# Two attentions with keys on partitions: the second shift products follow the scores at once, and keys are spread one batch ahead

## What is computed

```python
# first: 32 batches, 128 queries, 120 keys, 16 heads of 8 channels
attn = jnp.einsum('bhqd,bhkd->bhqk', q, k) * scale
attn = jnp.clip(attn, -CLAMP, CLAMP)
attn = jax.nn.softmax(attn, axis=-1)
...
x = jnp.einsum('bhqk,bhkd->bqhd', attn, v).reshape(B, Nq, Cq)
return x @ Wo + bo

# second: 128 queries, 128 keys, 16 heads of 4 channels, causal
scores = jnp.einsum('bhqd,bhkd->bhqk', q, k) / jnp.sqrt(jnp.float32(HD))
scores = jnp.where(causal, scores, -jnp.inf)
attn = jax.nn.softmax(scores, axis=-1)
o = jnp.einsum('bhqk,bhkd->bhqd', attn, v).transpose(0, 2, 1, 3).reshape(b, s, L)
x = x + o @ w_up
```

## Time and profile before

| | |
|---|---|
| median of 3 runs | 2061.7 us (2058.45 to 2063.37) |
| the profiled execution, its time | 2061.81 us |
| its span in the profile | 2060.0 us, granted TensorE clock 0.928 |
| TensorE busy (weight loads) | 1802.4 us, 87% (1398.8, 68%) |
| VectorE busy | 1510.3 us, 73% |
| GpSimd busy | 1177.6 us, 57% |
| ScalarE busy | 1112.8 us, 54% |

### The profile page before, as it was taken

How to read it: one execution, slowest core, us unless ns; L and a number is a source line. 1 busy time by engine, 2 the same in 40 slices (tenths; PEclk the granted TensorE clock), 3 DMA queues, 4 the chain that set the end, 5 groups by cost and what they waited for, 6 DMA issues and landing times. The chain is left out here.

```text
span 2060.0 us, 40382 instructions
## 1 busy us (share of the span) xinstructions
PE 1802.4 (87%) x12276; PEld 1398.8 (68%) x12306; DVE 1510.3 (73%) x3109; ACT 1112.8 (54%) x2864; POOL 1177.6 (57%) x1241
## 2 busy tenths in 40 slices
PE   3678767799999999986999999997778887799998
PEld 2355546588888888864888888885444444588886
DVE  5698868677787787777666666666668886677876
ACT  1366645555555555543666666664346565555554
POOL 3666637467776777654333333334767773677764
PEclk9799976799999999985999999998879997699999
DMA  5111100455565555410000000000000000212222
GB/s 122 46 44 40 42 25 11 113 137 138 144 144 145 125 148 145 128 60 3 5 4 3 4 4 3 4 3 1 0 1 1 0 0 16 60 61 83 81 63 71
DMA packets 99991, 114.77 MB, mean 56 GB/s; under 512 B 18448, under 2 KB 55504, under 8 KB 99888
## 3 DMA queue, kind: packets, MB, share of 16 engines
q1 hardware_dynamic: 96960, 112.14, 20.6%
q10 hardware_dynamic: 2928, 1.39, 0.3%
HBM read 101.82 MB, written 3.28 MB: 51 GB/s over the span
## 5 line engine op out<-in xcount | busy, mean ns | idle before, releaser
L76 POOL TENSOR_TENSOR b_moe_hid_low<-b_moe_hid,b_moe_hid_high 128x512 fp32r<-128x512 f32 x256 | 331.9, 1296 | 172.0 <-ACT b_moe_hid_high L1027 168.4
L1033 ACT ACTIVATE bank<-bank 128x512 f32<-128x512 f32 x384 | 223.5, 582 | 341.3 <-PE bank L83 341.3
L1729 POOL TENSOR_TENSOR c_prob<-c_prob,c_recip 128x480 f32<-128x480 f32 x128 | 126.3, 987 | 294.0 <-DVE c_recip L1877 294.0
L1835 ACT ACTIVATE c_prob<-bank,c_shift 128x120 f32<-128x120 f32 x512 | 177.9, 360 | 169.7 <-DVE c_shift L1869 169.7
L1058 DVE TENSOR_TENSOR b_moe_gu<-bank,XC 128x512 f32<-128x512 f32 x256 | 176.7, 690 | 114.8 <-PE bank L83 99.0
L76 POOL TENSOR_TENSOR e_moe_hid_low<-e_moe_hid,e_moe_hid_high 128x512 fp32r<-128x512 f32 x128 | 165.9, 1296 | 83.5 <-ACT e_moe_hid_high L1027 82.8
L71 DVE CAST c_ts_high<-bank 128x480 fp32r<-128x480 f32 x128 | 84.2, 658 | 153.2 <-PE bank L1760 153.2
L1063 DVE TENSOR_TENSOR b_moe_hid<-bank,b_moe_gu 128x512 f32<-128x512 f32 x256 | 177.0, 691 | 8.9 <-POOL b_moe_hid_low L76 0.3
L1027 ACT ACTIVATE b_moe_hid_high<-b_moe_hid 128x512 fp32r<-128x512 f32 x256 | 159.7, 624 | 9.8 <-DVE b_moe_hid L1063 9.0
L1760 PE MATMUL bank<-c_cs,mT 96*128 96x120 f32 x1024 | 142.2, 283 | 6.2 <-POOL c_wvp_low L76 4.8
L1760 PEld LDWEIGHTS bank<-c_cs,mT 96*128 96x128 f32 x1024 | 132.8, 196 | 20.8 <-DVE c_ts_low L76 9.7
(11 more groups left out here) (372 smaller groups left out, 5490.4 us busy)
## 6 DMA issues: line engine op xcount, KB each, us to landing
XC<-b_comb SPq DMA_DIRECT2D x256, 256.0 KB, 4.3
XC<-e_comb SPq DMA_DIRECT2D x64, 256.0 KB, 3.1
X<-in_x SPq DMA_DIRECT2D x4, 512.0 KB, 9.1
a_att_qs_high<-XC SPq DMA_DIRECT2D x32, 64.0 KB, 1.8
a_att_qs_low<-a_Q_low SPq DMA_DIRECT2D x32, 64.0 KB, 1.9
a_att_ks_high<-a_K_high SPq DMA_DIRECT2D x32, 64.0 KB, 1.9
a_att_ks_low<-a_K_low SPq DMA_DIRECT2D x32, 64.0 KB, 1.9
b_moe_w_gate<-in_b_wgT SPq DMA_DIRECT2D x8, 256.0 KB, 2.8
```

What stands on the lines that cost most here:

```text
L76: return eng.tensor_tensor(low.bitcast(F32R), x, high, ALU.subtract)
L1033: act.activation(gate_b[j % 4][:], gate_b[j % 4][:], ACT.Silu).then_inc(s_silu, 1)
L1729: pool.tensor_tensor(prob[k][:], prob[k][:], recip[:, k, :].unsqueeze(2).broadcast_to([P, HG, NKV]), ALU.mult).then_inc(s_norm, 1)
L1835: i = act.activation(prob[k][:, h, :], score_b[g % 2][:, h * NKV:(h + 1) * NKV], ACT.Exp, bias=shift[:, k, h:h + 1], accum_out=sums[:, k, ...
```

## The change

On TensorE shift B moves up to stand directly behind the second phase, the projection comes next and the turn of the heads last before the values products. The turned heads now go to `side_b`, columns 256 to 383, instead of `out_b`. So the values products wait for the heads to have been read (`s_heads`) and no longer for the copy of the turned ones; the turn of the row maxima, which writes the same bank as the turned heads, waits for last round's copy; and VectorE's addition, which reads that bank, waits for this round's copy. The projection now comes behind a wait for the spread row maxima of its own round, which it had before as well.

On ScalarE exponential B and the copy of turned heads change places. On GpSimd the low parts and `kd` are taken out of batch b's part and put in front of it for batch b+1; those of batch 0 come ahead of the loop.

```diff
+                    def spread_keys(b, v):
+                        if clamp:
+                            pool.wait_ge(s_place[v], (b - v) * 16 + 64)
+                        else:
+                            low_parts(b, v)
+                            pool.wait_ge(s_low, b + 1)
+                        wait(pool, s_second, b - 1)
+                        for part in range(2):
+                            i = pool.tensor_tensor(kd[v % 2][part][:].bitcast(F32R),
...
+                        i.then_inc(s_kd, 1)
+                    spread_keys(0, 0)
                     def body(b, v):
                         u = v % 2
+                        if has(b + 1):
+                            spread_keys(b + 1, (v + 1) % 4)
                         if has(b):
-                            if clamp:
-                                pool.wait_ge(s_place[v], (b - v) * 16 + 64)
...
                             wait(pool, s_first, b + 1)
...
                         if has(t - 1):
                             pe.wait_ge(s_mz, mz_steps * t)
                             wait(pe, s_out, t - 5)
+                            wait(pe, s_headT, t - 4)
                             pe.transpose(side_b[:, 0:P], mz[1 - u][:], ident[:]).then_inc(s_mt, 1)
...
-                        if has(t - 4):
-                            pe.wait_ge(s_heads, t - 3)
-                            pe.transpose(out_b[:, 0:P], heads[u][:], ident[:]).then_inc(s_ht, 1)
+                        if has(t - 2):
+                            pe.wait_ge(s_inB, t - 1)
+                            shift(u, (2, 3)).then_inc(s_shB, 1)
+                        if has(t - 1):
+                            pe.wait_ge(s_mrow, t)
                         if has(t - 5):
                             pe.wait_ge(s_headT, t - 4)
                             wait(pe, s_out, t - 5)
-                            if has(t - 1):
-                                pe.wait_ge(s_mrow, t)
                             pe.matmul(side_b[:, P:P + D], headT[1 - u][:], wo[:], start=True, stop=True).then_inc(s_y, 1)
-                        if has(t - 2):
-                            pe.wait_ge(s_inB, t - 1)
-                            shift(u, (2, 3)).then_inc(s_shB, 1)
+                        if has(t - 4):
+                            pe.wait_ge(s_heads, t - 3)
+                            pe.transpose(side_b[:, 2 * P:3 * P], heads[u][:], ident[:]).then_inc(s_ht, 1)
                         if has(t - 3):
                             pe.wait_ge(s_vprep, t - 2)
                             pe.wait_ge(s_expB, t - 2)
-                            wait(pe, s_headT, t - 3)
+                            wait(pe, s_heads, t - 3)
...
                             i.then_inc(s_mrow, 1)
+                        if has(t - 2):
+                            act.wait_ge(s_shB, t - 1)
+                            exps(u, 1).then_inc(s_expB, 1)
                         if has(t - 4):
                             act.wait_ge(s_ht, t - 3)
                             wait(act, s_y, t - 5)
-                            act.activation(headT[u][:], out_b[:, 0:P], ACT.Copy).then_inc(s_headT, 1)
-                        if has(t - 2):
-                            act.wait_ge(s_shB, t - 1)
-                            exps(u, 1).then_inc(s_expB, 1)
+                            act.activation(headT[u][:], side_b[:, 2 * P:3 * P], ACT.Copy).then_inc(s_headT, 1)
...
                         if has(t - 5):
                             dve.wait_ge(s_y, t - 4)
+                            if has(t - 4):
+
+                                dve.wait_ge(s_headT, t - 3)
```

More of the change, by code:

```diff
@@ L479, in low_parts @@
                         keep_low(pool, qs[v][1][:], Q[:, bass.ds(b * P, P)], qs[v][0][:]).then_inc(s_low, 1)
+                    def spread_keys(b, v):
[7 more added lines that the diff above has]
+                            i = pool.tensor_tensor(kd[v % 2][part][:].bitcast(F32R),
+                                                   ks[v][part][:, 0:nk].unsqueeze(1).broadcast_to([P, HG, nk]),
+                                                   headsel[:].unsqueeze(2).broadcast_to([P, HG, nk]), ALU.mult)
+                        i.then_inc(s_kd, 1)
+                    spread_keys(0, 0)
                     def body(b, v):
                         u = v % 2
+                        if has(b + 1):
+                            spread_keys(b + 1, (v + 1) % 4)
                         if has(b):
-                            if clamp:
-                                pool.wait_ge(s_place[v], (b - v) * 16 + 64)
-                            else:
-                                low_parts(b, v)
-                                pool.wait_ge(s_low, b + 1)
-                            wait(pool, s_second, b - 1)
-                            for part in range(2):
-                                i = pool.tensor_tensor(kd[u][part][:].bitcast(F32R),
-                                                       ks[v][part][:, 0:nk].unsqueeze(1).broadcast_to([P, HG, nk]),
-                                                       headsel[:].unsqueeze(2).broadcast_to([P, HG, nk]), ALU.mult)
-                            i.then_inc(s_kd, 1)
                             wait(pool, s_first, b + 1)
```

## The result

The kernel with the change takes 2017.96 us (2014.34 to 2018.92, 4 runs) against 2062.53 us (2058.45 to 2065.47, 4 runs) of the kernel before: ratio 0.9775, 95% interval 0.9762 to 0.9788. The profiled execution took 2014.34 us, with a span of 2012.6 us and a mean granted TensorE clock of 0.935 (before: 2060.0 us, 0.928). The two spans differ by 47.4 us, and that is the difference explained here.

The account below looks back on a forecast made before the run. Bounds: a loop of waits over heads and shift B in the first attention, GpSimd in the second. Gains 8.1 + 14.0 + 4.0 = 26.1 us took 2061.8 to 2035.7, forecast 2036 us, range 2024 to 2045.

Parts of the forecast that it names:

- the sign: Whole kernel: faster at chance 0.93, same 0.02, slower 0.05.
- A new neighbour for VectorE: First attention: small row-maxima limit waits for GpSimd's second key product; rounds alternate near 5.6 and 6.2 us, gain 8.1 us.
- The rounds at lower clock: First attention: three rounds at lower clock, as before the change, add 3.2 us.
- TensorE's queue in the second attention: Second attention: with keys spread ahead, TensorE is last at 6.5 us a round, gain 14.0 us.
- The ends: Last and filling rounds, both attentions: projection and shift B run inside the heads wait; gain 4.0 us, bounds 0 and 6.
- (d): Both attentions: the new rhythm keeps TensorE's clock low, 64 us more, 2126 us; chance 0.05.
- (a): First attention: the limit does not collide with GpSimd, gain 15.9 us there, 2028 us in all; chance 0.34.
- (b): First attention: limit sometimes waits for a second GpSimd product too, costing the whole gain there; 2044 us; chance 0.13.
- (c): Second attention: GpSimd stays last if the casts come later than read; gain 12, 2050 us; chance 0.05.
- Waits that were moved: Row-maxima turn, output sum, projection and values products: moved waits cost nothing, with about 0.7 us cover at the output sum.

Follow-up runs that it names:

- Keys as before: Changed kernel, but GpSimd spreads keys and queries of one batch together as in the kernel before, in both attentions: 2035.66 us, ratio 0.986.
- keys ahead alone: Kernel before with only GpSimd's part of the change, keys spread one batch ahead, TensorE and ScalarE untouched: 2057.18 us, ratio 0.9965.
- the limit first: Changed kernel, but VectorE handles the row maxima ahead of the clamp or mask of half A: 2030.7 us, ratio 0.9839.

## Why the prediction was wrong in size

The loops and their order were read rightly: the waits for heads and keys went, TensorE's queue became last in the second attention (two products instead of three: 6.16 to 5.78 us a round; in the first it was VectorE's, level with TensorE's in the forecast), the limit met the keys, rounds alternate, and the sign held. The forecast of 26.1 us is short of the 47.4 us between the two spans by 21.3, in four terms.

- **The price of one collision** (*A new neighbour for VectorE*). Places and times came as worked out: keys from F+4.91 to F+6.85, the limit's turn at F+6.21. But I let the limit begin when GpSimd ends, and it ends when GpSimd ends: it is delayed by 0.37 us (0.66 - 0.29), not by the 0.65 that I had (6.23 - 5.58), and with 0.15 to 0.26 us of a product left not at all. The pair at 279.16 in the earlier trace rows, a limit over the end of a short copy, fits that reading too; it was no case against a collision. With 5.52 us for the round without it (VectorE's queue; I had 5.53, and TensorE's 5.58 on top) the mean is 5.73, not 5.88: 26 x 5.88 - 148.9 = 4.0 us. "Keys as before" shows it from the other side: 5.52 once the collision is gone.
- **The rounds at lower clock**, 3.2 us, taken to stay as they were. The granted clock of the stretch rose from 0.97 to 1.00 and they are gone. That came with TensorE's and ScalarE's new order: "keys as before" has none of them, "keys ahead alone" has six. In the second profile of the same program the clock was 0.99, with one such round (6.43 us), behind one of 6.67 us at full clock that the limit's 1.13 us made; so this term is worth 2 to 3 us from run to run.
- **TensorE's queue in the second attention**, taken as 6.5 us, measured 6.16: 26 x 0.34 = 8.8 us. The first half was right (2.99 forecast, 2.92 measured; 1.34, measured 1.36 from 1609.38 to 1610.74). Behind shift B I had 0.43 + 0.49 + 1.18 = 2.10 us; it is 1.86 (1610.74 to 1612.60). The 0.43 was the distance from shift B to the next product in the old order of the first attention. There it is still 0.43, to the projection too (232.02 to 232.45), where the phase's products do not run straight into it; in the second attention shift B now follows the phase without a pause, and the distance is 0.32, as shift A's was there before (1544.81 to 1545.13). The 0.49 for projection and turned heads is 0.53 (0.32 + 0.21). To the 1.08 us of the values products, a drawn length, I had added 0.1 although neighbours overlap; from their start to the next round's it is 1.01. And 0.07 is the step from 6.43 to "6.5 for the small gaps", which the distances from start to start had in them already.
- **The ends**, 4.0 us, bounds 0 and 6; it is 10.9 us in the two ends. TensorE's time outside products went in the first from 6.6 to 5.2 us (26.77 - 20.16 and 21.07 - 15.87), 1.4 us, the wait that I had priced (2.0). The other 4.3 us are the same 209 products, faster: 20.16 to 15.87 us busy. Before, the granted clock was 0.74 and 0.76 in the ends, that is, about half of each at 1.2 GHz; with the new order it is 1.00, all at 2.4 GHz. The last rounds in the old order bring back 0.75 and 0.77, and 4.6 and 4.1 us. The clock does fall with the new order as well, only later. Before, it fell 13.1 us behind the last row maximum of the first attention, at 287.1 (1.00 up to there, 0.50 from there to 300.80), and 13.6 us behind that of the second; with the change it fell at 281.4, when the stage's last output sum was over, and at 1684.3, together with it. Over the profiles without work added on GpSimd, the six ends in the old order have it 12.6 to 14.6 us behind the last row maximum, and ten of the twelve in the new order 20.2 to 23.4; the other two have 14.4 and 14.8 (the second profile of the change and "the limit first"). I had used the clock only as a danger, rival (d); the same rows could have told of a gain, since the clock was under 1 before. The windows of the ends would have shown it, and I had not read them.

The remainder, 1.6 us the other way, is the filling of the pipelines and the other stages, 1.5 us of it behind the second attention, where the change does nothing; a single profile does not tell it from chance. In sum: 4.0 + 3.2 + 8.8 + (10.9 - 4.0) - 1.6 = 21.3.

**The rivals.** (a) would have been nearer in time (2028) for a wrong reason: the collision is there. (b) came true in part: in the first profile the limit always got through at the end of the product it met, but in the second it was held over a second product once in the 26 rounds (1.13 us at 133.10, with 0.06 us of the key product left and the queries' product next), and the two runs with more GpSimd work show it for longer. That round took 6.67 us instead of 5.9, far from the whole gain. (c) fell: GpSimd waits 0.9 us a round. (d) did not come; but keys ahead alone, with clock 0.94 and six rounds of 7.3 to 7.6 us, shows that a rhythm can bring it. Waits that were moved cost nothing seen in the rounds, as forecast.

The range was too narrow because the terms erred on one side together: to each queue something was added for safety, the collision was priced at the full length that was left, and the clock was held at its value of before.

## What to carry to other kernels

Add up a queue from distances from start to start in the new order's own pairs, those with a pause ahead of them kept apart from those without, and add nothing on top: gaps are in them. Where a change closes waits of TensorE, read the granted clock of every stretch that has them, the ends of pipelines too, and the moment at which it falls; where that lies inside the stretch, a closed wait can give its own length and the slowed products behind it (here 1.4 and 4.3 us). Before work is moved on GpSimd, look which small VectorE instruction between two SBUF tiles will lie beside it, and on which engine's queue the delay falls: where another engine was last the usual round did not change (6.16 us in "keys ahead alone"), where VectorE was last, it grew by all of it.

## What was not expected of the hardware

- A limit of 128 x 16 elements, 0.28 us alone, took up to 0.80 us beside a GpSimd product of 0.99 us, and 0.75 us in nearly every round when the keys alone were moved. It ends with the GpSimd instruction rather than beginning there. With 0.15 to 0.26 us of it left it was not delayed; with 0.06 us left and the next product right behind, it was held for that one too (1.13 us), and so it was by products drawn 0.05 us behind its own start (1.12 and 1.13 us). Products that began 0.14 us or more behind its start did not hold it when nothing held it already.
- It can be kept out for several GpSimd instructions that follow each other without a pause: 7.63 us beside seven of them, and 8.46 us with two fills among them.
- A fill, which reads nothing, keeps back the limit's end (1.30 us), but not the start of VectorE's next instruction (0.19 us behind the limit's); beside a product that reads, the next one started 1.34 us behind.
- In the second attention the split's subtraction (L76, 128 x 16 elements) took 0.38 us in its median, 0.18 with the keys as before. It costs nothing there, as TensorE is last: in "the limit first" it was 0.18 us too, and the round stayed at 6.17 us.
- The order of four rounds moved the moment at which the granted clock fell, by 7 and 11 us, and with it the clock of a stretch of 21 to 26 us: 1.00 with the new order, 0.74 to 0.77 with the old one, in both attentions. In a second profile of the changed kernel it was 0.81 in the first attention and 0.97 in the second, so the new order does not hold it in every run.
